# Moments of four normalizations in a fused graph-network kernel: from VectorE's closing instructions to GpSimd

## The reference, cut to what matters

```python
h = jnp.maximum(_layernorm(x, axis=-1), 0.0)          # "cheb" in the kernel
x = x + _L3_gnn_ref(h, adj, adj, ...)
...
xp = jnp.einsum('mn,bnf->bmf', L_norm, x)
h = _layernorm(xp @ Wc + bc, g1, be1)                 # "n1"
x1 = jax.nn.relu(h) + x
...                                                   # four-head masked attention on x1
x2 = _layernorm(x1 + o, g2, be2)                      # "n2"
m = jax.nn.gelu(x2 @ W1 + b1, approximate=False) @ W2 + b2
return _layernorm(x2 + m, g3, be3)                    # "n3"
```

## Time and profile before

| what | value |
|---|---|
| median of 3 runs | 1202.09 us (1201.91 to 1204.01) |
| span of the profiled execution | 1201.4 us |
| own time of the profiled execution beside its span | not given by the page; the median lies 0.7 us above the span |
| TensorE busy | 1124.4 us, 94% of the span |
| VectorE busy | 814.3 us, 68% |
| ScalarE busy | 759.7 us, 63% |
| GpSimd busy | 342.6 us, 29% |
| mean granted clock of TensorE | 0.978 of full speed |

### The profile page before, as it was taken

How to read it: one execution, slowest core, us unless ns; L and a number is a source line. 1 busy time by engine, 2 the same in 40 slices (tenths; PEclk the granted TensorE clock), 3 DMA queues, 4 the chain that set the end, 5 groups by cost and what they waited for, 6 DMA issues and landing times. The chain is left out here.

```text
span 1201.4 us, 23468 instructions
## 1 busy us (share of the span) xinstructions
PE 1124.4 (94%) x7537; PEld 898.6 (75%) x7537; DVE 814.3 (68%) x2964; ACT 759.7 (63%) x1627; POOL 342.6 (29%) x465
## 2 busy tenths in 40 slices
PE   8999999999999987999999999999999999999685
PEld 5678888889889865777777777777777777766454
DVE  7662222223335567798998988988988988977665
...
DMA packets 132321, 87.85 MB, mean 73 GB/s; under 512 B 13600, under 2 KB 115360, under 8 KB 132256
## 3 DMA queue, kind: packets, MB, share of 16 engines
...
...
## 5 line engine op out<-in xcount | busy, mean ns | idle before, releaser
L2247 DVE CUSTOM_DVE_ANT_0 att_Ts<-bank,mask_att 128x512 f32<-128x512 f32 x256 | 174.5, 683 | 63.6 <-PE bank L2402 61.2
L2149 ACT ACTIVATE att_Es<-att_Ts,att_small 128x512 f32<-128x512 f32 x256 | 185.4, 724 | 35.0 <-DVE att_small L2247 34.3
L2456 PE MATMUL bank<-ident,att_Es 128*128 128x128 f32 x1024 | 159.1, 279 | 16.8 <-ACT att_PTs L2158 12.3
L2158 ACT COPY att_PTs<-bank 128x512 f32<-128x512 f32 x248 | 144.0, 581 | 45.7 <-PE bank L2456 45.3
L2456 PEld LDWEIGHTS bank<-ident,att_Es 128*128 128x128 f32 x1024 | 121.7, 143 | 55.6 <-ACT att_PTs L2158 26.5
L2402 PE MATMUL bank<-K_parts,Q_parts 128*128 128x512 f32 x256 | 124.0, 494 | 3.7 <-DMA K_parts<-k_lo 2.3
L1943 POOL TENSOR_SCALAR n_rs<-n_mv 128x4 f32<-128x4 f32 x46 | 13.3, 289 | 306.4 <-DVE n_mv L1938 306.4
L985 DVE TENSOR_TENSOR P_row<-bank,l_bias 128x512 f32<-128x512 f32 x32 | 22.1, 691 | 86.1 <-PE bank L1440 68.0
L1430 PE MATMUL bank<-G,x0T 128*128 128x128 f32 x384 | 74.8, 276 | 0.7 <-DVE U2T L978 0.6
L1430 PE MATMUL bank<-G,U2T 128*128 128x128 f32 x384 | 74.2, 275 | 0.0
L1430 PE MATMUL bank<-G,U1T 128*128 128x128 f32 x384 | 74.2, 275 | 0.0
...
## 6 DMA issues: line engine op xcount, KB each, us to landing
Q_parts<-q_hi SPq DMA_DIRECT2D x128, 64.0 KB, 2.0
Q_parts<-q_lo SPq DMA_DIRECT2D x128, 64.0 KB, 2.0
K_parts<-k_hi SPq DMA_DIRECT2D x128, 64.0 KB, 2.0
K_parts<-k_lo SPq DMA_DIRECT2D x128, 64.0 KB, 2.0
...
```

Of the source, the lines that this page charges most:

```text
L2149: nc.scalar.activation(att_E[:, j % RING_E, :], att_T[:, j % RING_T, :], ACT.Exp, scale=-1.0, bias=att_small[:, 0, j:j + 1], accum_out=att ...
L2158: nc.scalar.copy(att_PT[:, h, :, cols(q)], c2[:].rearrange("p (s q) -> p s q", q=P)).then_inc(sem("att_pt"), 1)
L2247: nc.vector.tensor_tensor_reduce(att_T[:, j % RING_T, :], [c0, c1][j % 2][:], k.mask_att[:, tile_of(n, j)[1], :], -QK_SCALE, HUGE, ALU.add ...
L2456: mm = nc.tensor.transpose(dst[:, cols(s)], att_E[:, i % RING_E, cols(s)], k.ident[:])
```

## The change

cheb, n1, n2 and n3 lose the four `bn_aggr` per item on VectorE. In their place GpSimd puts mean and variance plus EPS together from the two halves' statistics, for all four tiles at once, with seven small instructions in four dependent stages (`ln_moments`). `ln_rstd` and `ln_scale_bias` call it in place of the wait and the EPS addition. The steps `cheb_aggr` and `n3_aggr` leave VectorE's lists; `n1_aggr` and `n2_aggr` become `n1_gain` and `n2_gain` in the same places and wait for GpSimd's mean. gat's and edge's normalizations stay, and so do the halves in which the last item's n2 and n3 are done. All other lists stay in their order.

```diff
-        def ln_aggr(dve, tag, n, last_reader):
-            stat, mv, _ = ln_mem[tag]
-            freed(dve, *last_reader)
-            ready_alone(dve, tag + "_stat", n, NT, NT)
-            for t in range(NT):
-                nc.vector.bn_aggr(mv[:, t, :], stat[:, t, :]).then_inc(sem(tag + "_aggr"), 1)
+        def ln_moments(pool, tag, n):
+
+            stat, mv, rs = ln_mem[tag]
+            half, spread = ln_half[tag], ln_spread[tag]
+            means = stat[:].rearrange("p t (u c) -> p t u c", c=3)[:, :, :, 1]
+            ready_alone(pool, tag + "_stat", n, NT, NT)
+            nc.gpsimd.tensor_scalar(half[:], means, 0.5, None, ALU.mult).then_inc(sem(tag + "_half"), 1)
+            nc.gpsimd.tensor_tensor(mv[:, :, 1], stat[:, :, 2], stat[:, :, 5], ALU.add).then_inc(sem(tag + "_half"), 1)
+            ready(pool, tag + "_half", n, 2, 2)
+            nc.gpsimd.tensor_tensor(mv[:, :, 0], half[:, :, 0], half[:, :, 1], ALU.add).then_inc(sem(tag + "_mean"), 1)
+            nc.gpsimd.tensor_tensor(spread[:], half[:, :, 0], half[:, :, 1], ALU.subtract
+                                    ).then_inc(sem(tag + "_spread"), 1)
+            nc.gpsimd.tensor_scalar(rs[:, 0, :], mv[:, :, 1], 1.0 / D, EPS, ALU.mult, ALU.add
+                                    ).then_inc(sem(tag + "_spread"), 1)
+            ready(pool, tag + "_spread", n, 2, 2)
+            nc.gpsimd.tensor_tensor(spread[:], spread[:], spread[:], ALU.mult).then_inc(sem(tag + "_square"), 1)
+            ready(pool, tag + "_square", n)
+            nc.gpsimd.tensor_tensor(rs[:, 0, :], rs[:, 0, :], spread[:], ALU.add).then_inc(sem(tag + "_vareps"), 1)
 
         def ln_rstd(pool, tag, n):
-            _, mv, rs = ln_mem[tag]
-            ready_alone(pool, tag + "_aggr", n, NT, NT)
-            nc.gpsimd.tensor_scalar(rs[:, 0, :], mv[:, :, 1], EPS, None, ALU.add).then_inc(sem(tag + "_vareps"), 1)
+            rs = ln_mem[tag][2]
+            ln_moments(pool, tag, n)
             ready(pool, tag + "_vareps", n)
...
         def ln_scale_bias(pool, tag, n):
...
-            ready_alone(pool, tag + "_aggr", n, NT, NT)
-            nc.gpsimd.tensor_scalar(rs[:, 0, :], mv[:, :, 1], EPS, None, ALU.add).then_inc(sem(tag + "_vareps"), 1)
+            ln_moments(pool, tag, n)
+            ready_alone(pool, tag + "_mean", n)
...
         def ln_gain(dve, tag, n, x, g):
             mv = ln_mem[tag][1]
-            ready(dve, tag + "_aggr", n, NT, NT)
+            ready(dve, tag + "_mean", n)
...
-            def n2_aggr(n):
-                ln_aggr(dve, "n2", n, ("n2_aff", n, NT))
+            def n2_gain(n):
                 ln_gain(dve, "n2", n, y2, "g2")
```

More of the change, by code:

```diff
@@ L1662 @@
     "DVE": """
[L1663 to L1668, removed]
+        cheb_stats gat_x2a+ att_rv+ gat_x2b+ gat_stats att_mask0 gat_aggr edge_stats att_mask1 edge_aggr gat_apply
+        cheb_lo att_scale att_mask2 att_mask3 ffn_y2 n2_stats n2_gain att_mask4 n2_apply cheb_y n1_stats att_mask5
+        gat_scores0 n1_gain att_mask6 n1_apply att_mask7 cheb_x1 gat_scores1 gat_scores2 ffn_y3 gat_scores3 att_mask8
+        gat_row1 gat_row2 gat_row3 gat_max0 gat_max1 att_mask9 gat_max2 edge_z gat_max3 edge_lc att_mask10 cheb_qlow
+        edge_max0 edge_max1 edge_max2 att_mask11 edge_max3 edge_le n3_stats att_mask12 edge_rden edge_attn cheb_klow
+        att_mask13 edge_u att_mask14 att_mask15 gat_rinv n3_apply edge_x3
     """.split(),
@@ L1713 @@
     "DVE": """
[L1714 to L1738, removed]
+        cheb_stats:0 gat_rinv:1 cheb_lo:0 gat_x2a:1 gat_x2b:1 gat_stats:2 gat_aggr:2 edge_stats:1 edge_aggr:1
@@ new lines @@
+        gat_apply:2 cheb_y:0 n1_stats:0 n1_gain:0 gat_scores0:2 n1_apply:0 gat_scores1:2 gat_scores2:2 cheb_x1:0
+        gat_scores3:2 gat_row1:2 gat_row2:2 gat_row3:2 gat_max0:2 gat_max1:2 gat_max2:2 gat_max3:2 edge_z:1 edge_lc:1
+        cheb_qlow:0 edge_max0:1 edge_max1:1 edge_max2:1 edge_max3:1 edge_le:1 cheb_klow:0 edge_rden:1 gat_rinv:2
+        edge_attn:1 edge_u:1 att_mask0:0 att_mask1:0 edge_x3:1 cheb_stats:1 gat_x2a:2 gat_x2b:2 gat_stats:3 gat_aggr:3
+        att_mask2:0 gat_apply:3 edge_stats:2 edge_aggr:2 att_mask3:0 att_mask4:0 cheb_lo:1 gat_scores0:3 gat_scores1:3
@@ new lines @@
+        edge_stats:3 att_mask1:1 edge_aggr:3 gat_apply:4 cheb_lo:2 att_scale:0 att_mask2:1 att_mask3:1 ffn_y2:0
+        n2_stats:0 n2_gain:0 att_mask4:1 n2_apply:0 gat_scores0:4 gat_scores1:4 att_mask5:1 gat_scores2:4
+        gat_scores3:4 cheb_y:2 gat_row1:4 n1_stats:2 gat_row2:4 att_mask6:1 n1_gain:2 gat_row3:4 gat_max0:4 ffn_y3:0
+        att_mask7:1 gat_max1:4 gat_max2:4 n1_apply:2 att_mask8:1 cheb_x1:2 edge_z:3 gat_max3:4 edge_lc:3 att_mask9:1
+        edge_max0:3 edge_max1:3 att_mask10:1 edge_max2:3 edge_max3:3 edge_le:3 n3_stats:0 att_mask11:1 cheb_qlow:2
@@ new lines @@
+        gat_rinv:4 edge_rden:3 edge_attn:3 att_mask12:1 edge_u:3 att_mask13:1 cheb_klow:2 n3_apply:0 att_mask14:1
+        att_mask15:1 att_rv:1 edge_x3:3 cheb_stats:3 gat_x2a:4 gat_x2b:4 edge_stats:4 gat_stats:5 gat_aggr:5
+        edge_aggr:4 att_mask0:2 att_mask1:2 cheb_lo:3 gat_apply:5 att_scale:1 att_mask2:2 ffn_y2:1 n2_stats:1
+        n2_gain:1 att_mask3:2 n2_apply:1 cheb_y:3 att_mask4:2 n1_stats:3 gat_scores0:5 gat_scores1:5 gat_scores2:5
+        gat_scores3:5 att_mask5:2 gat_row1:5 att_mask6:2 n1_gain:3 gat_row2:5 ffn_y3:1 gat_row3:5 gat_max0:5
@@ L1803 @@
     "DVE": """
[L1804 to L1818, removed]
@@ L1819 @@
-        n2_apply_0:15 n3_apply:14 att_scale_1:15 ffn_y2_1:15 n2_stats_1:15 n2_aggr_1:15 n2_gain_1:15 n2_apply_1:15
-        ffn_y3_0:15 n3_stats_0:15 n3_aggr_0:15 n3_gain_0:15 ffn_y3_1:15 n3_stats_1:15 n3_aggr_1:15 n3_apply_0:15
-        n3_gain_1:15 ffn_final_0:15 n3_apply_1:15 ffn_final_1:15
+        att_rv:12 gat_x2a:15 cheb_stats:14 gat_x2b:15 att_mask0:13 edge_stats:15 edge_aggr:15 att_mask1:13
+        att_mask2:13 att_scale:12 att_mask3:13 cheb_lo:14 ffn_y2:12 att_mask4:13 n2_stats:12 att_mask5:13 n2_gain:12
@@ new lines @@
+        att_mask6:13 n2_apply:12 att_mask7:13 cheb_y:14 n1_stats:14 n1_gain:14 att_mask8:13 att_mask9:13 n1_apply:14
+        cheb_x1:14 ffn_y3:12 n3_stats:12 att_mask10:13 att_mask11:13 edge_z:15 att_mask12:13 edge_lc:15 cheb_qlow:14
+        att_mask13:13 edge_max0:15 edge_max1:15 edge_max2:15 edge_max3:15 edge_le:15 att_mask14:13 cheb_klow:14
+        att_mask15:13 edge_rden:15 edge_attn:15 edge_u:15 n3_apply:12 att_rv:13 edge_x3:15 cheb_stats:15 att_mask0:14
+        att_mask1:14 att_scale:13 att_mask2:14 cheb_lo:15 ffn_y2:13 n2_stats:13 att_mask3:14 n2_gain:13 n2_apply:13
@@ new lines @@
+        cheb_y:15 att_mask4:14 n1_stats:15 n1_gain:15 att_mask5:14 n1_apply:15 att_mask6:14 cheb_x1:15 att_mask7:14
+        cheb_qlow:15 att_mask8:14 cheb_klow:15 att_mask9:14 att_mask10:14 ffn_y3:13 att_mask11:14 att_mask12:14
+        n3_stats:13 att_mask13:14 att_mask14:14 att_mask15:14 att_rv:14 n3_apply:13 att_mask0:15 att_mask1:15
+        att_mask2:15 att_scale:14 att_mask3:15 att_copy1:15 att_mask4:15 att_mask5:15 att_copy3:15 att_mask6:15
+        ffn_y2:14 att_mask7:15 n2_stats:14 att_copy5:15 n2_gain:14 att_rv_0:15 att_mask8:15 n2_apply:14 att_mask9:15
```

37 lines of the change are left out of this document (25 added, 12 removed).

## The result

The changed kernel takes **1226.46 us** (median of 4 runs, 1221.31 to 1228.65) against 1203.05 for the kernel before on the same chip: a ratio of 1.0193, 95% interval 1.0172 to 1.0214. It is slower, as forecast; 1232.5 was too high by 6 us, and the range of 1212 to 1248 holds the time.

What follows compares the result with a forecast made beforehand. TensorE sets the pace but stops whenever VectorE or ScalarE hand over late; 2.3 us a pass gives 23, plus fill 5.6 and drain 2, 30.6 on the 1201.4 span, median 0.7 above: 1232.5 us, range 1212 to 1248.

Steps and rivals of the forecast that it cites:

- VectorE relieved: Rival: no stall appears and sparing VectorE wins back a third of TensorE's idle time, 0.5 us a pass; 1197 us, chance 0.08.
- covered: Rival: lower-end price, with the sums vanishing in waits for transfers and in VectorE's margins; 1202 us, chance 0.05.
- the clock falls: Rival: TensorE's wait for gelu grows to about 2.1 us and work is paid twice; 1250 us, chance 0.06.
- The chain: GpSimd's seven small steps replacing one EPS addition in each normalization: +1.71 us until the power of -1/2.
- 2 x 0.31 + 5 x 0.28: GpSimd's new steps: two tensor_scalar at 0.31 and five tensor_tensor at 0.28 us, 2.02 us before subtracting the old step.
- The lower end of +1.2: Lowest price of GpSimd's steps, from bare instruction durations without gaps: +1.2 us.
- The 0.33 us beside VectorE's gains: In n2 and n1, four GpSimd steps running beside VectorE's gains lengthen by about 0.08 each, 0.33 us.
- The single row of the fill with 0.39: A GpSimd step beside VectorE's gains in the fill lasted 0.39 us; used for the upper price of the steps.
- The margins of 0.62 and 0.31 us: Slack absorbing delay: att_scale preceded TensorE's output projection by 0.62 us; VectorE waited 0.31 us before cheb_y.
- The walk with a chain of +1.2: Same delays at the lower price: 0.3 us at the projection, 0.5 after n2, 0.8 a pass; 1214 us.
- Fill and drain: Loss outside the loop: fill 5.6 us, at 1.4 a pass over four passes; drain an estimated 2 us.
- n1's queue behind b2: On GpSimd n1 starts only after the delayed b2 addition, making n1's shift another 0.6 us late.

Runs made afterwards that it cites:

- the run with the shorter chain: The changed kernel without the three steps that make the spread's part of the variance in each chain; 1208.37 us, ratio 1.0043.
- mask between: The changed kernel with attention mask 4 done between n2's statistics and n2's gain on VectorE in the loop; 1227.57 us, ratio 1.0192.
- low half late: The changed kernel with GpSimd's low half of the edge input waiting for VectorE's n2 shift in the loop; 1225.62 us, ratio 1.0199.
- n1 first: The changed kernel with n1's chain ahead of the b2 addition in GpSimd's queue, in the loop alone; 1226.06 us, ratio 1.0178.
- n1 alone: The changed kernel with only n1 closed by GpSimd's small steps, cheb, n2 and n3 closed by VectorE again; 1212.92 us, ratio 1.0087.

## Why the prediction was right, and by how much its terms were off

**The mechanism** held: gat_apply waits over 1 us for GpSimd, n2's gain begins 0.93 us after its statistics, its shift waits for the power, b2 and n1 stand back to back, n3 is free, the relief of VectorE ends in waits. *VectorE relieved* and *covered* are out by the ten passes; *the clock falls* by the granted clock of the loop. Two links ran otherwise. The prediction let cheb's delay reach TensorE at the projection; it arrives at gat's transposes, a margin that the prediction did not read. And it let the FFN transposes wait for n2's shift; they begin 0.44 us behind its end (862.77 to 863.21), late only by what TensorE had lost before.

**The chain** was mis-sized: +1.71 us forecast, +1.40 (n1, n2) and +1.45 (cheb) measured. The step was "2 x 0.31 + 5 x 0.28". The new steps take 1.77 up to the power in place of 2.02, for 0.22 of which the two short spacings stand (0.22 for 0.31, 0.15 for 0.28), and the step that went had taken 0.37 in n1 and n2, not 0.31. The lower end of +1.2 and the forecast enclose it.

**The 0.33 us beside VectorE's gains** did not appear: the three steps beside n2's gain (859.44 to 860.58) are 0.20 long and 0.28 apart like the others. The single row of the fill with 0.39 was not typical; in the run with the shorter chain one step of each n chain (849.20, 0.35 us) did show it.

**From link to link**, forecast against measured lateness: gat_apply +1.4, +1.30; projection +0.85, +0.60; n2's shift +2.26, +1.58; second FFN product +1.95, +1.18; n1's shift +2.55, +1.85; a pass +2.3, **+1.57**. The margins of 0.62 and 0.31 us that the prediction read fit the trace; most of the error is the chain's and the 0.33's, carried through. The walk with a chain of +1.2 had given 0.8 a pass, that with +1.71 2.3, and 1.4 lies between them as 1.57 does.

**Fill and drain**: 5.6 and 2 forecast, 6.3 and 2.2 measured; that they come so close is partly luck. Four of the profiled kernels have the same fill and drain and differ in the loop alone. Their fill, from the first cheb statistics to the first reciprocal, took 177.9 us (changed) and 178.4 (mask between) at a mean granted clock of 0.94, 177.1 (low half late) and 176.2 (n1 first) at 0.95, against 171.6 at 0.96 before: 4.6 to 6.8 more, part of it the clock's. Whether the longer waits lowered the clock is not shown. Their drain took 146.4 to 148.2 against 144.3. Sum: 15.7 + 6.3 + 2.2 = 24.2 in place of 30.6, to which the profiled execution adds 1.3 of the unchanged first part.

**Sub-additivity** is not in the prediction; the expectation ahead of n1 alone has it (0.8 alone, 0.4 in the full change). The prediction took n1's queue behind b2 as 0.6 on top of n2's delay; n1 alone costs 0.92, and on top of the others some 0.4 (1.57 - 0.67 - 0.50), because n2's delay of VectorE moves n1's statistics towards b2's end.
